# Graph network layer in split float32: where the second layer's weights start in a partition

## What is computed

```
h   = max(layernorm(x), 0)                                  # 50000 x 256
agg = segment_mean(edge_attr_64, dst)                       # 50000 x 64
hid = relu(concat([agg, h], axis=1) @ W1 + b1)              # 320 -> 512
out = x + hid @ W2 + b2                                     # 512 -> 256
```

## Time and profile before

| | us |
|---|---|
| median of 3 runs | 1345.34 (1344.73 to 1345.53) |
| profiled execution | 1346.03 |
| its span | 1344.4 |
| TensorE busy | 1326.3 (99%) |
| VectorE busy | 1216.8 (91%) |
| ScalarE busy | 696.2 (52%) |
| GpSimd busy | 541.7 (40%) |

### The profile page before, as it was taken

One profiled execution on the slowest core, in us unless ns is written; L12 is line 12 of the kernel. 1 busy time (PEld: TensorE's weight loads), 2 busy tenths in 40 slices (PEclk: granted clock), 3 DMA queues, 4 the chain that ended last, 5 costly groups with the idle time before them and its releaser, 6 DMA issues.

```text
span 1344.4 us, 29244 instructions
## 1 busy us (share of the span) xinstructions
PE 1326.3 (99%) x6976; PEld 1118.6 (83%) x6976; DVE 1216.8 (91%) x3153; ACT 696.2 (52%) x1285; POOL 541.7 (40%) x707
## 2 busy tenths in 40 slices
PE   6999999999999999999999999999999999999998
PEld 3788888888888888888888888888888888888887
DVE  6899999999999999999999999999999999999997
ACT  5455555555555555555555555555555555555553
POOL 6443434343434343434343434343434343434341
PEclk9999999999999999999999999999999999999999
DMA  4676767676767676767676767676767666767663
GB/s 118 123 121 133 121 133 121 134 120 133 121 133 121 133 121 134 120 133 121 133 121 133 121 134 120 134 120 134 121 134 120 135 120 134 120 134 120 134 110 77
DMA packets 420692, 168.19 MB, mean 125 GB/s; under 512 B 319092, under 2 KB 420230, under 8 KB 420680
## 3 DMA queue, kind: packets, MB, share of 16 engines
q1 hardware_dynamic: 419688, 166.89, 66.8%
q10 hardware_dynamic: 992, 1.18, 0.3%
HBM read 66.25 MB, written 51.40 MB: 88 GB/s over the span
## 4 chain that ended last, share of the span: by engine, by line
PE 94%; SPq 2%; DVE 1%; DMA 1%; issue 1%; POOL 0%; ACT 0%; DVEq 0%; POOLq 0%
PE P L932 26%; PE P L934 13%; PE P L909 13%; PE P L911 13%; PE P L910 13%; PE P L918 6%; PE P L919 6%; PE PA L898 1%; PE PA L897 1%; DMA X<-in_x_dram 1%; SPq L322 0%; SPq L323 0%; SPq L310 0%; PE PA L893 0%; DMA dst_w<-in_dst_dram 0%
## 5 line engine op out<-in xcount | busy, mean ns | idle before, releaser
L932 PE MATMUL P<-w_both,H_hi 128*128 128x512 f32 x1564 | 558.8, 398 | 2.2 <-DVE H_lo L729 2.1
L611 ACT ACTIVATE H_hi<-P 128x512 fp32r<-128x512 f32 x392 | 233.1, 596 | 496.8 <-PE P L919 496.8
L934 PE MATMUL P<-w_both,H_lo 128*128 128x256 f32 x1564 | 440.3, 282 | 0.0
L932 PEld LDWEIGHTS P<-w_both,H_hi 128*128 128x128 f32 x1564 | 294.4, 188 | 75.5 <-DVE H_lo L729 3.2
L729 DVE SCALAR_TENSOR_TENSOR H_lo<-P,H_hi 128x512 fp32r<-128x512 f32 x392 | 266.4, 680 | 76.2 <-ACT H_hi L611 73.1
L909 PE MATMUL P<-HT_hi,w_hi 128*128 128x512 f32 x776 | 308.3, 397 | 0.0
L911 PE MATMUL P<-HT_hi,w_lo 128*128 128x512 f32 x776 | 304.3, 392 | 0.0
L910 PE MATMUL P<-HT_lo,w_hi 128*128 128x512 f32 x776 | 302.1, 389 | 0.0
L460 POOL TENSOR_TENSOR XB<-X,b_row 128x1024 f32<-128x1024 f32 x97 | 233.5, 2407 | 168.4 <-DVE O L743 165.9
L934 PEld LDWEIGHTS P<-w_both,H_lo 128*128 128x128 f32 x1564 | 294.2, 188 | 3.8
L454 POOL TENSOR_TENSOR E_both<-ES,E_both 128x256 fp32r<-128x256 f32 x98 | 72.9, 744 | 390.7 <-ACT E_both L591 390.7
(11 more groups left out here) (85 smaller groups left out, 1190.7 us busy)
## 6 DMA issues: line engine op xcount, KB each, us to landing
out_dram<-O SPq DMA_DIRECT2D x97, 512.0 KB, 4.6
HQ<-HN SPq DMA_DIRECT2D x384, 128.0 KB, 4.1
X<-in_x_dram SPq DMA_DIRECT2D x95, 512.0 KB, 4.3
ER<-in_edge_attr_dram SPq DMA_DIRECT2D x392, 32.0 KB, 1.8
DT<-table_dram SPq DMA_DIRECT2D x392, 1.0 KB, 1.7
X<-in_x_dram ACTq DMA_DIRECT2D x1, 512.0 KB, 5.0
w_raw<-in_L_gnn_W_dram ACTq DMA_DIRECT2D x4, 128.0 KB, 5.0
w_raw<-in_L_gnn_W_dram SPq DMA_DIRECT2D x2, 256.0 KB, 4.5
```

What stands on the lines that cost most here:

```text
L611: act.activation(H1_hi[:, m, nodes(t)], bank(m)[:, nodes(t)], ACT.Relu).then_inc(s_1hi, 1)
L932: pe.matmul(out_bank(j)[some, :], H1_hi[:, m, rows], w2_both[:, m, :, :].rearrange("p a d -> p (a d)"), start=(m == 0), stop=False)
L934: last = pe.matmul(out_bank(j)[some, 0:D], H1_lo[:, m, rows], w2_both[:, m, 0, :], start=False, stop=(m == CH - 1))
```

## The change

Two unused tensors are named, one in front of w2_both and one behind it. `beside_w` takes 24 float32, 96 bytes, in each partition, `beside_x` takes 8, 32 bytes. No instruction reads or writes either.

```diff
         ab_hi = sb("ab_hi", [P, H], F32R)
+        beside_w = sb("beside_w", [P, 24])
         w2_both = sb("w2_both", [P, CH, 2, D], F32R)
+        beside_x = sb("beside_x", [P, 8])
```

## The result

The changed kernel takes 1351.14 us (median of 6 runs, 1350.46 to 1352.03), the kernel before 1345.43 in the same measurement: a ratio of 1.0041, with an interval of 1.0031 to 1.0051. It is slower by 5.7 us. The forecast was 1336 us, 9.4 less than before.

What follows compares the result with a forecast made beforehand. TensorE's distance from one matmul to the next was taken as the bound. The second layer's 9.4 us less, all else 0, off the median 1345.34 gave 1336 us; range 1330 to 1357, the forecast's own 1330 to 1342.

Steps and rivals of the forecast that it cites:

- everything behind w2_both: Tensors behind w2_both, first layer's moving operands included, move up 128 bytes, keeping their start modulo 128; priced at nothing.
- the rival of the 128 bytes behind: First layer's 3112 matmuls change if the pattern exceeds 128 bytes: 19 us slower, to 1364, or 9 us less; chance 0.10.
- the straddle: Moving stream of w2_both touches one more 64-byte group per matmul: 10.6 us slower, 1356, or 1366 at both; chance 0.22.
- The term of the sum: Second layer's 512-column matmul falls from 235 to 229 ns, the 256-column one stays: 6 x 1564 = 9.4 us less.
- 235 is the top of what this shape shows in this trace in steady running: Second layer's 512-column matmul, 235 ns to the next start: most other standings of the two streams shown are quicker.
- The other half of the reason: The same 512-column matmul takes about 229 ns where a tile's second layer begins, turning slow only in the third pair.
- The mechanism: Next weights' load and running matmul's moving stream obstruct each other by address and amount read: 6 ns of a pair.
- Nothing changes: Second layer: a start at 32 is as good or bad as one at 64; time stays at 1345.3 us; chance 0.26.
- The slack: VectorE's idle time, some 1.1 us a tile, exceeds TensorE's gain of 96 ns, so all should reach the end.

Runs made afterwards that it cites:

- e1: The kernel before with one gap of 128 bytes in front of w2_both and none behind it; 1358.15 us against 1346.08 for the kernel before.
- e3: The kernel before with gaps of 96 bytes in front of w2_both and 160 behind it; 1339.25 us, ratio 0.9949.
- e4: The kernel before with one gap of 128 bytes in front of w1_hi, so first-layer weights and all behind move together; 1346.26 us, ratio 1.0004.
- the map: Both layers' paces in kernels with different gaps, by D: moving operand's start less stationary one's, in bytes, modulo 256; times from 1339.3 to 1358.2 us.
- q2: The kernel before with the weight loads of six of a block's eight first-layer matmuls cut to the first 96 of 128 columns; 1355.12 us.
- q3: The kernel before with the weight loads of six of a block's eight first-layer matmuls cut to the last 96 of 128 columns; 1348.25 us.
- m1: The kernel before with 64 columns of weights in place of 128 in six of a block's eight first-layer matmuls; 1346.85 us (before: 1344.9).
- q1: The kernel before with the weight loads of six of a block's eight first-layer matmuls cut to the first 32 of 128 columns; 1351.83 us.
- s6: The kernel before with gaps of 128 bytes in front of w2_both and 32 behind it; 1350.2 us.
- q4: The kernel before with the moving operand of six of a block's eight first-layer matmuls standing still, weight loads full; 1317.75 us.
- f1: The kernel before with gaps of 160 bytes in front of w2_both and 32 behind it; 1347.23 us, ratio 1.0001.
- f2: The kernel before with gaps of 32 bytes in front of w2_both and 160 behind it; 1349.14 us, ratio 1.0018.
- m2: The weight loads cut as in m1, in the kernel with one gap of 128 bytes in front of w2_both; 1353.71 us.
- s2: The kernel before with no gap in front of w2_both and 64 bytes behind it; 1352.0 us.
- s1: The kernel before with no gap in front of w2_both and 192 bytes behind it; 1345.7 us.

## Why the prediction was wrong

**The step that failed** is "everything behind w2_both", which I priced at nothing because a pattern of 128 bytes sees no difference. In the first layer the pattern is 256 bytes long. It has its stationary operands in front of the gap and its moving ones behind it, so its distance changed from 64 to 192. That is the rival of the 128 bytes behind, at a chance of 0.10 (0.08 for slower) and a price of 19 us; it measured 4.4 x 3112 = 13.7 us by the paces, 12 us by e1's time (1358.15 - 1346.08), which has nearly the second layer of before. I had named it and written "For it nothing speaks but that no row excludes it"; the same could be said of the 128 bytes on which the sum stood. I had also priced forecast and rival as if only one could hold. Both did: 8.4 us less and 13.7 more, with half a microsecond in the edge sums, make 5.8, and 5.7 were measured. That 1351 lies inside the range of 1330 to 1357 is luck: the upper part of the range was there for the straddle, which did not happen.

**The term of the sum was right in sign and nearly in size.** I took 6 ns off the pair and 9.4 us off the time. The pair fell by 5.4 ns, 8.4 us. e3, which keeps the gain and undoes the rest, measures 6.8 us less than before. But its reason was weak and partly chance. The other distances of the second layer lie from 346.7 to 352.5 ns, all below the 353 of before, so "235 is the top of what this shape shows in this trace in steady running" was a fair sign, and no more than that. The other half of the reason was misread: a duration of 0.39 us was taken for a quick place. The starts at the head of that tile's second layer, this row and the one at 708.00 of the earlier trace rows, are 0.71 us apart, 355 ns for each of the first two pairs:

```profile
707.29 0.39 PE L932 MATMUL P<-w_both,H_hi 128*128 128x512 f32 x1
```

Over the tiles of the loop the first pair takes 355 ns, the second 347 and the others 353. And the gain did not come as forecast, all in the 512-column matmul: L934 lost 4 ns of its mean and L936 2.

**The mechanism was half wrong.** That the distance of the two reads matters was right (e4, the map, q2 against q3). That the load costs by what it reads was wrong (m1, q1). I had drawn it from three pairs in the last tile, 347 ns with 80 columns against 352.5. By q1 to q3 such a load has its last column elsewhere, 192 bytes lower, and D counted from there is 128; but the map has 351 ns for that, so this doesn't explain the 347 either. The same three pairs in other kernels show how little they can carry. In the changed kernel and in e3 they take 345 and 347 ns, where pairs with full loads take 347.6 and 347.8, and in s6 they are slower, 1.06 / 3 = 353 ns against 347.2:

```profile
1343.90 0.40 PE L934 MATMUL P<-w_both,H_hi 128*80 128x512 f32 x1
...
1344.96 0.40 PE L934 MATMUL P<-w_both,H_hi 128*80 128x512 f32 x1
```

A shorter load doesn't save 6 ns whatever the addresses. What made it 347 before the change stays open. As for the rule in the Trainium skill, "TensorE: Matmul & The Clock Gate", section "Step-by-step: what each phase is for", that loads take no read bandwidth from the running matmul: m1 agrees that less load gives nothing back (229.0 ns both ways). The conclusion that I drew from it, that no address would matter, is refuted: the distance between the load and the moving operand is worth over 4 ns of 229 in the first layer. The same page gives N/2.4 + 2.5 ns in its section "Back-to-back issue gap" for an isolated matmul with N columns at the upper clock. For 512 columns that is 215.8 ns, and q4's six matmuls agree with 215.8; those whose operand walks don't: 231 to 233 ns in q4, and means of 228.4 and more in all other runs.

**The other rivals.** The straddle was expected to show as 405 ns in the 512-column group (now L934), or 289 in the 256-column one (now L936); 394 and 280 rule it out. "Nothing changes" fell with the rows of both layers.

**The slack.** That a gain of some 96 ns a tile would reach the end held for e3 (74 ns a tile, 6.8 us). With 100 in f1 it didn't, for a reason that stays open.

## What to carry to other kernels

Where float32r matmuls follow each other without a gap, as here at the upper clock, look at the distance between the moving and the stationary operand's starts, modulo 256 bytes: it was worth up to 5 ns of 233 in the first layer and 6 ns of 353 in the second, some 1% of the kernel between this version and the one of e3. A gap ahead of one tensor shifts all that is named behind it against all in front, so pad to a multiple of 256 in total if one tensor alone is to move. Then read every group of matmuls again, those that the edit doesn't name too, and repeat the time: f1 and f2 have the shortest median tiles and not the best times.

## What the runs showed of the hardware

- The excess of a float32r matmul over its columns (15.7 ns of 229) falls to 2.5 when its moving operand stands still: 215.8 ns (q4). Weight loads of 64 columns left it (m1) or took 1.1 ns (m2), loads of 32 columns gave 231.5 ns (q1).
- In the first layer the pace repeats with a distance of 256 bytes (before, e3), and the distance counts from the load's last column, not from its first (q2 232.1, q3 229.6). That would fit weights that are read from the end, which is not shown.
- One thing that I wasn't looking for. s2 moves HN and HQ, and X and O too, to multiples of 256 bytes (HN0 at 109824; before at 109760). The transfers' share of the 16 engines falls from 66.8% to 50.9%. The median time of one from HN to HQ falls from 4.1 to 3.2 us, of a load of X from 4.3 to 3.4, of a store of O from 4.6 to 3.3. The page of s2, queues and issues:

```profile
q1 hardware_dynamic: 419688, 166.89, 50.9%
```
```profile
HQ<-HN SPq DMA_DIRECT2D x384, 128.0 KB, 3.2
```

The pieces of that transfer are 256 bytes long, 64 float32 of a partition. At 128 modulo 256, in s1, the share was 68.7%. The Trainium skill's page "DMA: Bandwidth & Descriptors", section "How a descriptor splits into AXI transactions", says that a transaction must start at a multiple of 256 bytes, so that a piece which starts elsewhere begins with a transaction from the boundary below it. By that a piece of 256 bytes off the boundary takes two transactions for one; the shares of s1 and s2 agree in direction. Each is of a single execution. Little of it can reach the time here, since TensorE sets the end, and s2 is slower for its distances. A version with both, these transfers aligned and D at 64 and 32, wasn't tried.
